# Pool queue in runs of sixteen gathers and sixteen scatters, first edge of equal nodes found by the merging matmul

## The chip, the cores and the metric

One NeuronCore of one Trainium2 chip, float32 throughout. The metric is the device time of one execution in microseconds; the median of three runs is given, and one further execution was profiled.

## The reference

A graph layer over N = 3125 nodes with 160 features and E = 53125 edges (random, sorted by `dst`; every edge has a `src` and a `dst` node). In short:

```
h   = relu(layernorm(x))                      # [N, 64 scalars + 32 vectors of 3]
s,v = h_s @ W_nl0,  einsum(h_v, W_nl1)
w   = relu(edge_attr_64 @ W_fc1) @ W_fc2      # per edge: w0..w4
xs, xv = s[dst], v[dst]                       # gather per edge
tp  = [w0*xs, w3*dot(xv,sh1), w1*xs*sh1, w2*xv, w4*cross(xv,sh1)]
agg = segment_sum(tp, src) / 32               # scatter-add per edge
out = x + gated( agg @ W_out_s + h_s @ W_skip0,  agg @ W_out_v + h_v @ W_skip1 )
```

The kernel applies `W_out_*` to each edge's products before the sum over `src`, so one edge adds a row of M = 192 floats.

## The kernel before

**Tiling.** Edges go in 416 tiles of 128; 4 tiles are a group (104 groups, index g, place j in a group), 2 groups a block (52 blocks, index b). All engines walk over the groups in software pipelines, each with its own written-out order of steps; DVE, PE and ACT have loops, the queues of POOL and SP are fully unrolled.

**POOL** (lines 376 to 417) only issues indirect DMAs in the main part: `gathers(b)` reads for every tile of a block 128 rows of 160 floats from `node_table` into one of 16 group slots `rows`; `scatters(b)` adds for every tile 128 rows of 192 floats into one of three DRAM tables `sums[t]` (three, so that a scatter waits only for the third one before it: one table has one scatter in flight). The order is 7 blocks of gathers first, then for each b: gathers of block b + 7 (8 of them), scatters of block b (8). After block 44 no gathers are left and the last 64 scatters follow one another. In every fourth block one of the eight gathers is left to SP, which reads its 128 rows by single-row DMAs.

**SP** (lines 280 to 340) loads, for each block, `from_col` and `from_row` (the `src` numbers of the block, the latter broadcast to all partitions, 512 KB), `ef` (edge features, 256 KB), and then issues 32 of those single-row reads (`gather_rows`, line 329) in blocks 0 to 47. `load_from(b)` waits for the indices of block b - 2 (`idx_ready`), because its buffers are double.

**DVE** (lines 794 to 930) makes the edge products from the gathered rows, adds the radial parts, and prepares the scatter. In a scatter, no row may occur twice: `same_nodes` builds per tile the 128x128 matrix `same` (line 872: equal `src` or not) and, by a second instruction (line 873, `before`), counts how many equal nodes stand before each edge. `repeats` and `rows_to_add` turn that into `add_idx`: the node for the first edge of equal nodes, a dump row for the others. `rows_to_add` (line 897) waits until the scatters that last used the index slot have landed (`added`), 8 groups earlier.

**PE** computes the hidden layers and the outputs, and `merge` (line 538) multiplies `same` with the messages, so that the first edge of equal nodes holds their sum. **ACT** copies PSUM results; `collect` (line 652) copies the merged sums into `to_add`, a ring of 8 groups, after the scatters that last used the slot have landed.

**At the end** SP reads the three tables back, and they are added, gated and stored.

Of the kernel before, what the change touches and what calls it, by code (L numbers as in the profile page):

```python
# [15 lines left out]
ALU = mybir.AluOpType  # L16
# [5 lines left out]
P = 128  # L22
N = 3125
E = 53125
S, V = 64, 32
# [37 lines left out]
W_LT = W_MC + 3 * V  # L63
W_DUMP = W_LT + P
W_END = W_DUMP + 1
# [19 lines left out]
EARLY_GROUPS = 2  # L85
AHEAD = 7
# [8 lines left out]
PER_BLOCK = [len(range(t, 2 * J, TABLES)) for t in range(TABLES)]  # L95
# [3 lines left out]
def table_of(b, p):  # L99

    turn = 2 * (b - DRAIN) if isinstance(b, int) and b > DRAIN else 0
    return (p + turn) % TABLES


def scattered(t, b, p):

    if isinstance(b, int) and b > DRAIN:
        return PER_BLOCK[t] * DRAIN + sum(table_of(k, q) == t for k in range(DRAIN, b + 1)
                                          for q in range(2 * J if k < b else p))
    return PER_BLOCK[t] * b + sum(q % TABLES == t for q in range(p))  # L110

# [35 lines left out]
def build_program(nc, x, wpack, edge_t, nodes_to, nodes_from, nodes_row, nodes_by_row, edge_vec, out):  # L147
# [3 lines left out]
    with ExitStack() as ctx:  # L151
# [11 lines left out]
        lower = w[:, W_LT:W_LT + P]  # L163
# [4 lines left out]
        spare = sb("spare", [P, max(NT * (S + M + 3 * V), UNROLL * J * (G_END + M))])  # L168
# [25 lines left out]
        msg = sb("msg", [P, 2, J, OUTS])  # L194
        radial = sb("radial", [P, 2, 2, 3 * V])
        same = sb("same", [P, 2, J, P])
        before = sb("before", [P, J, P])
        key = sb("key", [P, 3, 2, J])
        to_add_0 = sb("to_add_0", [P, UNROLL, J, M])
        to_add_1 = spare[:, UNROLL * J * G_END:UNROLL * J * (G_END + M)].rearrange(  # L200
# [5 lines left out]
        vec = msg[:, :, :, :].rearrange("p k j f -> p (k j f)")[:, 0:3 * TILES].rearrange("p (t i) -> p t i", i=3)  # L206
# [49 lines left out]
        def landed(b, u, j):  # L256

            p = u % 2 * J + j
            t = table_of(b, p)
            return t, 16 * scattered(t, b, p + 1)  # L260
# [6 lines left out]
        def _(sp):  # L267
# [95 lines left out]
        def _(pool):  # L363
# [29 lines left out]
            def scatters(b, v):  # L393

                for h in range(2):
                    pool.wait_ge(idx_ready, 2 * b + h + 1)
                    for j in range(J):
                        p = h * J + j
                        t = table_of(b, p)
                        if j % 2 == 0:  # L400
                            pool.wait_ge(sums_ready, 4 * b + 2 * h + 1 + j // 2)
                        if scattered(t, b, p) == 0:
                            pool.wait_ge(zeroed, 16 * (2 * len(ZERO_RUNS) + 1))
                        else:
                            pool.wait_ge(added[t], 16 * scattered(t, b, p))
                        pool.indirect_dma_start(  # L406
                            sums[t], bass.IndirectOffsetOnAxis(ap=add_idx[:, 2 * v + h, j:j + 1], axis=0),
                            to_add[2 * v + h][:, j, :], None, compute_op=ALU.add,
                        ).then_inc(added[t], 16)
# [4 lines left out]
            for b in range(BLOCKS):  # L414
                if b + AHEAD < BLOCKS:
                    gathers(b + AHEAD, (b + AHEAD) % ROWS_LOOP)
                scatters(b, b % LOOP)

        @block.tensor
        def _(pe):  # L420
# [107 lines left out]
            def merge(g, u, m):  # L528

                if not valid(g, GROUPS):  # L530
                    return
                pe.wait_ge(msg_ready, 2 * g + m + 1)
                if m == 0:
                    pe.wait_ge(same_ready, g + 1)
                if valid(g - 1, GROUPS) or m == 1:
                    pe.wait_ge(sums_ready, 2 * g + m)
                for q in range(2):
                    ins = nc.tensor.matmul(d_ps[:, q * M:(q + 1) * M], same[:, u % 2, 2 * m + q, :],  # L538
                                           msg[:, u % 2, 2 * m + q, 0:M], start=(q == 0), stop=(q == 1),
                                           skip_group_check=True)  # L540
                ins.then_inc(summed, 1)
# [35 lines left out]
        def _(act):  # L577
# [66 lines left out]
            def collect(g, u, m, b):  # L644
# [7 lines left out]
                nc.scalar.activation(to_add[u][:, 2 * m:2 * m + 2, :],  # L652
                                     d_ps[:, 0:2 * M].rearrange("p (q o) -> p q o", q=2),
                                     ACT.Copy).then_inc(sums_ready, 1)

            def step(i, u):
                g = RING * i + u
                u1, u2, u3 = (u - 1) % RING, (u - 2) % RING, (u - 3) % RING
                b3 = LOOP * i + (u - 3) // 2
# [3 lines left out]
                collect(g - 3, u3, 0, b3)  # L663
# [4 lines left out]
                collect(g - 3, u3, 1, b3)  # L668
# [28 lines left out]
        def _(dve):  # L697
# [78 lines left out]
            def vector_lengths():  # L776
# [8 lines left out]
                dve.wait_ge(rhat_ready, 1)  # L785

# [73 lines left out]
            def same_nodes(g, u, i):  # L860
# [5 lines left out]
                if valid(g - 2, GROUPS):  # L866
                    dve.wait_ge(summed, 2 * g - 2)
                    dve.wait_ge(idx_ready, g - 1)
                for j in range(J):
                    row = from_row[:, par, (h * J + j) * P:(h * J + j + 1) * P]  # L870
                    col = from_col[:, par, h * J + j:h * J + j + 1]
                    nc.vector.tensor_scalar(same[:, k, j, :], row, col, None, ALU.is_equal)  # L872
# [3 lines left out]
                nc.vector.tensor_scalar(key[:, 1, k, :], from_col[:, par, h * J:(h + 1) * J], -1.0,  # L876
                                        w[:, W_DUMP:W_DUMP + 1], ALU.mult, ALU.add).then_inc(same_ready, 1)

            def repeats(g, u):
                if not valid(g, GROUPS):  # L880
                    return
                k = u % 2
                dve.wait_ge(same_ready, g + 1)
                nc.vector.scalar_tensor_tensor(key[:, 2, k, :], key[:, 0, k, :], 0.5, key[:, 1, k, :],
                                               ALU.is_gt, ALU.mult).then_inc(repeats_ready, 1)

            def rows_to_add(g, u, b):

                if not valid(g, GROUPS):
                    return  # L890
                par, h, k = u // 2 % 2, u % 2, u % 2
                dve.wait_ge(repeats_ready, g + 1)
                if valid(g - RING, GROUPS):
                    for j in range(J - TABLES, J):
                        t, n = landed(b - LOOP, u, j)
                        dve.wait_ge(added[t], n)
                nc.vector.tensor_tensor(add_idx[:, u, :], key[:, 2, k, :], from_col[:, par, h * J:(h + 1) * J],  # L897
                                        ALU.add).then_inc(idx_ready, 1)

            def step(i, u):  # L900
                g = ROWS_RING * i + u
                u2 = (u - 2) % RING
# [7 lines left out]
                early = isinstance(g, int) and g - 2 < EARLY_GROUPS  # L910
                if not early:
                    same_nodes(g - 2, u2, 2 * i + (u - 2) // RING)
                radial_part(g - 2, u2, 1)
                if not early:
                    repeats(g - 2, u2)
                vectors(g - 2, u2, 1)
                if not early:
                    rows_to_add(g - 2, u2, 2 * LOOP * i + (u - 2) // 2)

            def early_group(g):  # L920
                same_nodes(g, g, 0)
                repeats(g, g)
                rows_to_add(g, g, g // 2)

            early_group(0)
# [3 lines left out]
            early_group(1)  # L929
# [5 lines left out]
            for u in range(SKEW, GROUPS % ROWS_RING + TAIL - 2):  # L935
                step(GROUPS // ROWS_RING, u)
# [41 lines left out]
def pack_weights(skip0, skip1, nl0, nl1, fc1, fc2, out_s, out_v):  # L978
# [34 lines left out]
    put(0, W_LT, np.tril(np.ones((P, P), np.float32), -1))  # L1013
    w[:, W_DUMP] = NPAD + np.arange(P)
    return w
# [40 lines left out]
```

## Time and profile before

| | us |
|---|---|
| median of 3 runs (1382.02 to 1385.59) | 1385.2 |
| profiled execution | 1387.66 |
| its span | 1385.8 |
| POOL busy | 1066.5 |
| PE busy / DVE busy / ACT busy | 919.5 / 880.1 / 428.5 |

The span is the time from the first to the last recorded instruction. Busy time of POOL is the time inside its DMA instructions; each is preceded by about 0.3 us that count as idle, so start-to-start distances say more than busy times. "idle before <-X" names what the engine had waited for last; "issue" means nothing that the profile shows.

### The profile page before, as it was taken

The numbers are of one execution on the slowest core, as the hardware profiler recorded it, in microseconds if no ns is written. First come the engines' busy times: TensorE is split into PE (matmuls) and PEld (weight loads), VectorE is DVE, ScalarE is ACT, GpSimd is POOL, SyncE is SP. The second block draws the span as 40 slices with busy tenths as digits, with TensorE's granted clock in tenths as the row PEclk, the third lists the DMA queues.
The fourth block names the chain that finished last, engine by engine and source line by source line (L and its number), as shares of the span: only waits on it lengthen the run. The fifth ranks groups of instructions, "written<-read, shape, count | busy, mean of one in ns | idle before, by whom it ended". The sixth has DMA issues, their size and how long they took to land.

```text
span 1385.8 us, 26047 instructions
## 1 busy us (share of the span) xinstructions
PE 919.5 (66%) x5648; PEld 780.3 (56%) x5648; DVE 880.1 (64%) x3693; ACT 428.5 (31%) x839; POOL 1066.5 (77%) x830
## 2 busy tenths in 40 slices
PE   7498766757757768577677675776766757769103
PEld 5387655646646657466566574665655646658102
DVE  7899747657566576575675766656647667579105
ACT  5154332322323323223233232232332323325101
POOL 1777788888888888888878888788788887887880
PEclk9699877786877877778778787787787877779556
DMA  9635555555454555554555555545554555456557
GB/s 351 165 92 102 105 80 86 99 80 105 81 80 105 78 84 101 80 105 80 80 105 80 88 97 81 104 79 82 105 78 88 97 80 106 79 78 90 52 55 274
DMA packets 124075, 139.89 MB, mean 101 GB/s; under 512 B 34241, under 2 KB 99585, under 8 KB 123970
## 3 DMA queue, kind: packets, MB, share of 16 engines
q0 software_dynamic: 79296, 74.04, 38.2%
q1 hardware_dynamic: 44674, 64.92, 15.1%
q14 instruction: 97, 0.79, 0.2%
q8 instruction: 8, 0.13, 0.0%
HBM read 86.24 MB, written 52.66 MB: 100 GB/s over the span
## 4 chain that ended last, share of the span: by engine, by line
DMA 31%; POOL 26%; DVE 23%; issue 14%; PE 3%; DVEq 2%; ACT 0%; POOLq 0%; SPq 0%; ACTq 0%
DMA sums<-to_add,add_idx 15%; DMA sums<-spare,add_idx 15%; POOL turn_space L388 9%; POOL sums L406 8%; DVE products_space L805 6%; POOL rows L388 5%; POOL spare L388 5%; DVE products_space L834 4%; DVE before L873 2%; DVE same L872 2%; DVE products_space L832 2%; DVE products_space L831 2%; DVE radial L847 1%; DVE msg L858 1%; DVE turn_space L816 1%
## 5 line engine op out<-in xcount | busy, mean ns | idle before, releaser
L507 PE MATMUL t_ps<-w,products_space 128*128 128x128 f32 (+1 forms) x1248 | 225.2, 312 | 350.6 <-DVE products_space L834 350.6
L523 PEld LDWEIGHTS o_ps<-w,pT 128*128 128x128 f32 (+1 forms) x2496 | 360.5, 223 | 40.7 <-issue 37.9
L406 POOL DMA_INDIRECT sums<-to_add,add_idx x208 | 326.6, 1570 | 67.9 <-issue 47.3
L507 PEld LDWEIGHTS t_ps<-w,products_space 128*128 128x128 f32 (+1 forms) x1248 | 166.3, 160 | 373.7 <-issue 335.8
L523 PE MATMUL o_ps<-w,pT 128*128 128x96 f32 (+1 forms) x2496 | 376.6, 309 | 0.0
L406 POOL DMA_INDIRECT sums<-spare,add_idx x208 | 326.6, 1570 | 64.4 <-issue 46.0
L631 ACT ACTIVATE pT<-t_ps 128x512 f32<-128x512 f32 (+1 forms) x312 | 185.4, 594 | 320.2 <-PE t_ps L507 319.7
L897 DVE TENSOR_TENSOR add_idx<-key,from_col 128x4 int32<-128x4 f32 x104 | 16.9, 163 | 371.0 <-DMA sums<-spare,add_idx 206.7
L388 POOL DMA_INDIRECT turn_space<-node_table,to_idx x186 | 187.1, 1006 | 56.7 <-issue 46.7
L640 ACT ACTIVATE msg<-o_ps 128x448 f32<-128x448 f32 x208 | 113.0, 543 | 335.8 <-PE o_ps L523 327.4
L538 PE MATMUL d_ps<-msg,same 128*128 128x192 f32 x832 | 197.0, 365 | 28.4 <-ACT spare L652 20.6
L538 PEld LDWEIGHTS d_ps<-msg,same 128*128 128x128 f32 x832 | 153.2, 217 | 60.9 <-issue 60.9
L388 POOL DMA_INDIRECT rows<-node_table,to_idx x112 | 114.2, 1020 | 41.3 <-issue 27.4
L491 PE MATMUL w_ps<-w,hid 64*128 64x224 f32 x832 | 145.4, 482 | 0.7 <-ACT hid L623 0.7
L873 DVE SCALAR_TENSOR_TENSOR before<-from_row,from_col,w 128x128 f32<-128x128 int32 x416 | 142.9, 343 | 0.0
L388 POOL DMA_INDIRECT spare<-node_table,to_idx x106 | 105.7, 997 | 32.4 <-issue 25.7
L872 DVE TENSOR_SCALAR same<-from_row,from_col 128x128 f32<-128x128 int32 x416 | 126.3, 305 | 0.0
L491 PEld LDWEIGHTS w_ps<-w,hid 64*128 64x128 f32 x832 | 93.9, 245 | 31.4 <-issue 26.6
L652 ACT ACTIVATE spare<-d_ps 128x384 f32<-128x384 f32 x104 | 51.1, 491 | 128.3 <-DMA sums<-spare,add_idx 105.3
L847 DVE TENSOR_TENSOR radial<-msg,rhat 128x192 f32<-128x192 f32 x208 | 72.5, 349 | 26.5 <-ACT msg L640 26.5
L805 DVE TENSOR_TENSOR products_space<-turn_space,rhat 128x256 f32<-128x256 f32 (+2 forms) x240 | 78.4, 392 | 3.5 <-issue 1.3
L652 ACT ACTIVATE to_add<-d_ps 128x384 f32<-128x384 f32 x104 | 51.1, 491 | 72.3 <-DMA sums<-to_add,add_idx 57.1
(96 smaller groups left out, 865.6 us busy)
## 6 DMA issues: line engine op xcount, KB each, us to landing
from_row<-nodes_row SPq DMA_DIRECT2D x52, 512.0 KB
ef<-edge_t SPq DMA_DIRECT2D x52, 256.0 KB
turn_space<-node_table SPq DMA_DIRECT2D x768, 0.6 KB
spare<-node_table SPq DMA_DIRECT2D x768, 0.6 KB
turn_space<-sums SPq DMA_DIRECT2D x9, 480.0 KB, 7.0
sums<-zeros SPq DMA_DIRECT2D x6, 672.0 KB, 9.2
sums<-to_add,add_idx POOLq DMA_INDIRECT x208, 3.6
sums<-spare,add_idx POOLq DMA_INDIRECT x208, 3.6
```

The costliest lines, as they stand in the source:

```text
L388: pool.indirect_dma_start(rows[2 * v + h][:, j, SC:CR], None, table, bass.IndirectOffsetOnAxis(ap=to_idx[:, (2 * b + h) * J + j:(2 * b + h ...
L406: pool.indirect_dma_start(sums[t], bass.IndirectOffsetOnAxis(ap=add_idx[:, 2 * v + h, j:j + 1], axis=0), to_add[2 * v + h][:, j, :], None, ...
L491: ins = nc.tensor.matmul(w_ps[m][:, q * NFC2:(q + 1) * NFC2], hid[half, par, cols], w[half, W_FC2:W_FC2 + NFC2], start=(q == 0), stop=(q = ...
L507: ins = nc.tensor.transpose(t_ps[(3 * u + c) % 2][0:ROWS[c], j * P:(j + 1) * P], prod[:, u % 2, j, a:e], ident)
L523: ins = nc.tensor.matmul(o_ps[m][:, base + oc:base + oc + n], pT[c][u % 2][:, cols], w[0:ROWS[c], wc:wc + n], start=(q == 0 and c == 0), s ...
L538: ins = nc.tensor.matmul(d_ps[:, q * M:(q + 1) * M], same[:, u % 2, 2 * m + q, :], msg[:, u % 2, 2 * m + q, 0:M], start=(q == 0), stop=(q ...
L631: nc.scalar.activation(pT[c][u % 2][:], t_ps[(3 * u + c) % 2][0:ROWS[c], :], ACT.Copy).then_inc(pT_ready, 1)
L640: nc.scalar.activation(msg[:, u % 2, 2 * m:2 * m + 2, :], o_ps[m][:, 0:2 * OUTS].rearrange("p (q o) -> p q o", q=2), ACT.Copy).then_inc(ou ...
L652: nc.scalar.activation(to_add[u][:, 2 * m:2 * m + 2, :], d_ps[:, 0:2 * M].rearrange("p (q o) -> p q o", q=2), ACT.Copy).then_inc(sums_read ...
L805: ins = nc.vector.tensor_tensor(vecs(crs[:, dst, :, i0 * V:(i0 + n) * V], n), vecs(rows[u][:, :, VE + v0 * V:VE + (v0 + n) * V], n), unit( ...
L872: nc.vector.tensor_scalar(same[:, k, j, :], row, col, None, ALU.is_equal)
L873: nc.vector.scalar_tensor_tensor(before[:, j, :], row, col, lower, ALU.is_equal, ALU.mult, accum_out=key[:, 0, k, j:j + 1])
```

## The change

1. **POOL order.** Blocks are taken in runs of two: gathers of blocks run + 7 and run + 8 (sixteen, or fifteen where SP takes one), then the scatters of blocks run and run + 1 (sixteen). The rotation over the three tables continues inside a run and restarts at each run.
2. **SP.** Before the loads of block b + 1, from b = 5 on, SP waits until all scatters of a whole run have landed: `scatters_landed((b - 5) // 2 * 2 + 1)`. `load_from(b)` itself waits for `same_ready` in place of `idx_ready`.
3. **First edge.** The `before` instructions are gone. A column of ranks, 3^(63-p) for edge p, stands ahead of each message; `merge` multiplies 193 columns in place of 192, `collect` copies the summed rank along, and `repeats` compares it with twice the edge's own rank. `repeats` and `rows_to_add` move from g - 2 to g - 4 in the step of DVE, and `rows_to_add` no longer waits for `added`.
4. `to_add` has 16 + 192 floats for each row; scatters read its last 192.

```diff
-            for b in range(BLOCKS):
-                if b + AHEAD < BLOCKS:
-                    gathers(b + AHEAD, (b + AHEAD) % ROWS_LOOP)
-                scatters(b, b % LOOP)
+            for run in range(0, BLOCKS, RUN):
+                for b in range(run + AHEAD, min(run + AHEAD + RUN, BLOCKS)):
+                    gathers(b, b % ROWS_LOOP)
+                for b in range(run, run + RUN):
+                    scatters(b, b % LOOP)
...
+            def scatters_landed(b):
+
+                for t in range(TABLES):
+                    sp.wait_ge(added[t], 16 * scattered(t, b, 2 * J))
+
             for b in range(BLOCKS):
+                if b + 1 < BLOCKS and b > LOOP:
+                    scatters_landed((b - LOOP - 1) // RUN * RUN + RUN - 1)
                 if b + 1 < BLOCKS:
                     load_from(b + 1, (b + 1) % 2)
...
                 if valid(b - 2, BLOCKS):
-                    sp.wait_ge(idx_ready, 2 * b - 2)
+                    sp.wait_ge(same_ready, 2 * b - 2)
...
-                    nc.vector.scalar_tensor_tensor(before[:, j, :], row, col, lower, ALU.is_equal, ALU.mult,
-                                                   accum_out=key[:, 0, k, j:j + 1])
...
             def repeats(g, u):
...
+                dve.wait_ge(sums_ready, 2 * g + 2)
+                nc.vector.scalar_tensor_tensor(key[:, 1, u % UNROLL, :], to_add[u][:, :, SUM_AT - 1],
+                                               w[:, W_FIRST:W_FIRST + 1], key[:, 0, u % UNROLL, :],
+                                               ALU.is_le, ALU.mult).then_inc(repeats_ready, 1)
...
-                if valid(g - RING, GROUPS):
-                    for j in range(J - TABLES, J):
-                        t, n = landed(b - LOOP, u, j)
-                        dve.wait_ge(added[t], n)
-                nc.vector.tensor_tensor(add_idx[:, u, :], key[:, 2, k, :], from_col[:, par, h * J:(h + 1) * J],
-                                        ALU.add).then_inc(idx_ready, 1)
+                nc.vector.tensor_scalar(add_idx[:, u, :], key[:, 1, u % UNROLL, :], -1.0, w[:, W_DUMP:W_DUMP + 1],
+                                        ALU.mult, ALU.add).then_inc(idx_ready, 1)
```

## Rows read from the trace of the kernel before

**Rows 1.** The page's first lines: span, and busy time of each engine (share, instructions).
```profile
span 1385.8 us, 26047 instructions
PE 919.5 (66%) x5648; PEld 780.3 (56%) x5648; DVE 880.1 (64%) x3693; ACT 428.5 (31%) x839; POOL 1066.5 (77%) x830
```

**Rows 2.** Part 5, POOL's DMA instructions: count, busy us, mean ns, idle before, releaser.
```profile
L406 POOL DMA_INDIRECT sums<-to_add,add_idx x208 | 326.6, 1570 | 67.9 <-issue 47.3
L406 POOL DMA_INDIRECT sums<-spare,add_idx x208 | 326.6, 1570 | 64.4 <-issue 46.0
...
L388 POOL DMA_INDIRECT turn_space<-node_table,to_idx x186 | 187.1, 1006 | 56.7 <-issue 46.7
...
L388 POOL DMA_INDIRECT rows<-node_table,to_idx x112 | 114.2, 1020 | 41.3 <-issue 27.4
```

**Rows 3.** The view of waits: us in total, times, longest.
```profile
DVE add_idx L897 <- DMA sums<-spare,add_idx: 206.7, 25, 9.7
```

**Rows 4.** Timeline of POOL: start, us, line, tile, idle before; first, turnarounds, last.
```profile
36.07 1.15 POOL L388 DMA_INDIRECT rows<-node_table,to_idx  x1 [7.48 <-DMA node_table<-spare]
...
614.10 1.56 POOL L406 DMA_INDIRECT sums<-spare,add_idx  x1 [0.30 <-issue]
615.97 1.02 POOL L388 DMA_INDIRECT spare<-node_table,to_idx  x1 [0.30 <-DMA sums<-spare,add_idx]
...
625.08 1.61 POOL L406 DMA_INDIRECT sums<-to_add,add_idx  x1 [0.30 <-issue]
...
640.15 1.02 POOL L388 DMA_INDIRECT turn_space<-node_table,to_idx  x1 [0.30 <-DMA sums<-to_add,add_idx]
...
650.63 1.62 POOL L406 DMA_INDIRECT sums<-to_add,add_idx  x1 [0.30 <-issue]
...
1350.01 1.55 POOL L406 DMA_INDIRECT sums<-spare,add_idx  x1 [0.30 <-issue]
```

**Rows 5.** The view of line 406: from a scatter's issue to its landing.
```profile
DMA to landing us min/median/max: 3.5/3.6/7.8
```

**Rows 6.** Timeline of SP's queue: the loads of two following blocks, and a late one.
```profile
108.71 0.42 SPq L289 DMA_DIRECT2D from_row<-nodes_row  x1
...
110.99 14.37 SPq L329 DMA_DIRECT2D turn_space<-node_table  x32
...
125.83 0.45 SPq L289 DMA_DIRECT2D from_row<-nodes_row  x1
...
646.47 0.43 SPq L289 DMA_DIRECT2D from_row<-nodes_row  x1
```

**Rows 7.** Windows of 1 us after the load at 618.82: engines' busy, PEclk, DMA share, GB/s.
```profile
622.00:623.00 1.00, 1.00 (x6) 1.00 (x5) 1.00 (x3) 0.58 (x1) 0.69 (x2) 0.63 0.95 344
...
626.00:627.00 1.00, 1.00 (x10) 0.72 (x11) 1.00 (x7) 0.71 (x2) 0.69 (x1) 1.00 0.02 4
```

**Rows 8.** Timeline of POOL around the load at 125.83.
```profile
125.68 1.56 POOL L406 DMA_INDIRECT sums<-to_add,add_idx  x1 [0.30 <-DMA sums<-to_add,add_idx]
...
129.41 1.56 POOL L406 DMA_INDIRECT sums<-to_add,add_idx  x1 [0.30 <-issue]
133.52 1.56 POOL L406 DMA_INDIRECT sums<-to_add,add_idx  x1 [2.55 <-DMA sums<-to_add,add_idx]
```

**Rows 9.** Timeline in the last 64 scatters: two loads and the stalls behind them.
```profile
1247.18 0.43 SPq L289 DMA_DIRECT2D from_row<-nodes_row  x1
...
1252.98 1.69 POOL L406 DMA_INDIRECT sums<-to_add,add_idx  x1 [1.22 <-ACT to_add L652]
...
1263.04 0.43 SPq L289 DMA_DIRECT2D from_row<-nodes_row  x1
...
1269.16 1.55 POOL L406 DMA_INDIRECT sums<-spare,add_idx  x1 [1.29 <-DMA sums<-spare,add_idx]
```

**Rows 10.** The removed instruction on the page, and once beside a gather.
```profile
L873 DVE SCALAR_TENSOR_TENSOR before<-from_row,from_col,w 128x128 f32<-128x128 int32 x416 | 142.9, 343 | 0.0
...
644.16 0.40 DVE L873 SCALAR_TENSOR_TENSOR before<-from_row,from_col,w 128x128 f32<-128x128 int32 x1
644.24 0.95 POOL L388 DMA_INDIRECT turn_space<-node_table,to_idx  x1 [0.30 <-issue]
```

More of the change, by code:

```diff
@@ L62 @@
 W_MC = W_MB + 3 * V
-W_LT = W_MC + 3 * V
-W_DUMP = W_LT + P
-W_END = W_DUMP + 1
+W_DUMP = W_MC + 3 * V
+W_RANK = W_DUMP + 1
+W_FIRST = W_RANK + 1
+W_END = W_FIRST + 1
 NA = W_NC - W_NA
@@ L85 @@
 EARLY_GROUPS = 2
+SUM_AT = 16
+SUM_ROW = SUM_AT + M
 AHEAD = 7
@@ L92, with scattered_in_runs @@
 TAIL = 4
-PER_BLOCK = [len(range(t, 2 * J, TABLES)) for t in range(TABLES)]
+RUN = 2
+PER_RUN = [len(range(t, RUN * 2 * J, TABLES)) for t in range(TABLES)]
 DRAIN = BLOCKS - AHEAD
 def table_of(b, p):
-    turn = 2 * (b - DRAIN) if isinstance(b, int) and b > DRAIN else 0
+    turn = 2 * (b % RUN) if b <= DRAIN else 2 * (DRAIN % RUN + b - DRAIN)
     return (p + turn) % TABLES
 def scattered(t, b, p):
[L107 to L110, printed above, removed]
+    return sum(table_of(k, q) == t for k in range(b + 1) for q in range(2 * J if k < b else p))
+def scattered_in_runs(t, run, place):
+    return PER_RUN[t] * run + sum(q % TABLES == t for q in range(place))
 def last_place(t):
@@ L193, in build_program @@
         pT = [[sb(f"pT{c}{k}", [ROWS[c], GE]) for k in range(2)] for c in range(3)]
-        msg = sb("msg", [P, 2, J, OUTS])
+        ranked = sb("ranked", [P, 2, J, 1 + OUTS])
+        msg = ranked[:, :, :, 1:1 + OUTS]
         radial = sb("radial", [P, 2, 2, 3 * V])
         same = sb("same", [P, 2, J, P])
[L197 to L200, printed above, removed]
+        key = sb("key", [P, 2, UNROLL, J])
+        to_add_0 = sb("to_add_0", [P, UNROLL, J, SUM_ROW])
+        to_add_1 = spare[:, UNROLL * J * G_END:UNROLL * J * (G_END + SUM_ROW)].rearrange(
             "p (u j m) -> p u j m", u=UNROLL, j=J)
@@ L254, in build_program, with landed @@
         gates = to_add_0[:, :, :, :].rearrange("p u j m -> p (u j m)")[:, 0:NT * SO].rearrange("p (t s) -> p t s", s=SO)
[L256 to L260, printed above, removed]
+        def landed(run, u, j):
+            place = u % (2 * RUN) * J + j
+            if isinstance(run, int) and run > DRAIN // RUN:
+                b, p = divmod(run * RUN * 2 * J + place, 2 * J)
+                t = table_of(b, p)
+                return t, 16 * scattered(t, b, p + 1)
+            t = place % TABLES
+            return t, 16 * scattered_in_runs(t, run, place + 1)
         out_sb = rows_0[:, :, :, :].rearrange("p u j f -> p (u j f)")[:, 0:NT * F].rearrange("p (t f) -> p t f", t=NT)
@@ L537, in merge @@
                 for q in range(2):
-                    ins = nc.tensor.matmul(d_ps[:, q * M:(q + 1) * M], same[:, u % 2, 2 * m + q, :],
-                                           msg[:, u % 2, 2 * m + q, 0:M], start=(q == 0), stop=(q == 1),
+                    ins = nc.tensor.matmul(d_ps[:, q * (1 + M):(q + 1) * (1 + M)], same[:, u % 2, 2 * m + q, :],
+                                           ranked[:, u % 2, 2 * m + q, 0:1 + M], start=(q == 0), stop=(q == 1),
                                            skip_group_check=True)
@@ L642, in copy_outputs, with collect @@
                                      ACT.Copy).then_inc(out_copied, 1)
-            def collect(g, u, m, b):
+            def collect(g, u, m, run):
                 if not valid(g, GROUPS):
@@ L649, in collect @@
                     for j in (2 * m, 2 * m + 1):
[L650 removed]
+                        t, n = landed(run - LOOP // RUN, u, j)
                         act.wait_ge(added[t], n)
[L652 to L653 removed]
+                nc.scalar.activation(to_add[u][:, 2 * m:2 * m + 2, SUM_AT - 1:SUM_ROW],
+                                     d_ps[:, 0:2 * (1 + M)].rearrange("p (q o) -> p q o", q=2),
                                      ACT.Copy).then_inc(sums_ready, 1)
@@ L658, in step @@
                 u1, u2, u3 = (u - 1) % RING, (u - 2) % RING, (u - 3) % RING
-                b3 = LOOP * i + (u - 3) // 2
+                run = LOOP // RUN * i + (u - 3) // (2 * RUN)
                 copy_turned(g - 1, u1, 0)
@@ L662, in step @@
                 copy_turned(g - 1, u1, 1)
-                collect(g - 3, u3, 0, b3)
+                collect(g - 3, u3, 0, run)
                 copy_outputs(g - 2, u2, 1)
@@ L667, in step @@
                     hidden(LOOP * i + u // 2 + 1, (u // 2 + 1) % 2)
-                collect(g - 3, u3, 1, b3)
+                collect(g - 3, u3, 1, run)
             hidden(0, 0)
@@ L867, in same_nodes @@
                     dve.wait_ge(summed, 2 * g - 2)
-                    dve.wait_ge(idx_ready, g - 1)
+                if valid(g - UNROLL, GROUPS):
+                    dve.wait_ge(repeats_ready, g - UNROLL + 1)
                 for j in range(J):
-                    row = from_row[:, par, (h * J + j) * P:(h * J + j + 1) * P]
-                    col = from_col[:, par, h * J + j:h * J + j + 1]
-                    nc.vector.tensor_scalar(same[:, k, j, :], row, col, None, ALU.is_equal)
-                    nc.vector.scalar_tensor_tensor(before[:, j, :], row, col, lower, ALU.is_equal, ALU.mult,
-                                                   accum_out=key[:, 0, k, j:j + 1])
-                nc.vector.tensor_scalar(key[:, 1, k, :], from_col[:, par, h * J:(h + 1) * J], -1.0,
+                    nc.vector.tensor_scalar(same[:, k, j, :], from_row[:, par, (h * J + j) * P:(h * J + j + 1) * P],
+                                            from_col[:, par, h * J + j:h * J + j + 1], None, ALU.is_equal)
+                nc.vector.tensor_scalar(key[:, 0, u % UNROLL, :], from_col[:, par, h * J:(h + 1) * J], -1.0,
                                         w[:, W_DUMP:W_DUMP + 1], ALU.mult, ALU.add).then_inc(same_ready, 1)
@@ L934, in _ @@
                     step(i, u)
-            for u in range(SKEW, GROUPS % ROWS_RING + TAIL - 2):
+            for u in range(SKEW, GROUPS % ROWS_RING + TAIL):
                 step(GROUPS // ROWS_RING, u)
```

39 lines of the change are left out of this document (14 added, 25 removed).

## The prediction

> **What bounds the kernel now.** I read the busy times first [rows 1]: POOL leads with 1066.5 us, but 77% of a span bounds nothing by itself. The reader is to see why it does here in POOL's timeline [rows 4]: from the gather at 36.07 to the end of the scatter at 1350.01 + 1.55 = 1351.6, POOL issues one indirect DMA after another, each 0.30 us behind the one before. The 254 us that count as idle in these 1315.5 us are almost all that fixed 0.30. The page's groups [rows 2] give the pieces: 416 scatters of 1570 ns, 404 gathers of about 1008 ns (the third group, into the tile spare, is like the two shown). With the gap, an undisturbed scatter takes 1.55 + 0.30 = 1.86 us from start to start (the last scatter's duration in [rows 4]) and an undisturbed gather 0.95 + 0.30 = 1.25 [rows 10]. 416 x 1.86 + 404 x 1.25 = 1279; POOL's stretch is 1315.5, so all disturbances together are worth 36 us. That is the most that a new order of the same DMAs could win, and it is the account on which the change books.
>
> The waits agree: DVE stands 206.7 us at the index instruction for the landing of scatters out of the tile spare alone, half of the ring [rows 3], so compute runs ahead until the ring of eight groups is full and is then released by POOL. Ahead of 36 and after 1351.6 (34 us of reading back and finishing) nothing of the change matters: its additions there are one column instruction.
>
> **The change part by part.** Sums are against the profiled 1387.66 us (span 1385.8); the median of the runs is 2.5 lower, and I apply the difference to the median.
>
> *DVE without `before`, indices two groups later, one column more in merge and collect.* 416 x 343 ns = 143 us leave DVE [rows 10]. DVE waits for POOL, so the wait grows by as much: 0. The cover is POOL's pace of about 51 us for two blocks (625.08 to 650.63 is one [rows 4]). Do the later indices come in time? The indices of a run need DVE two groups beyond it, and those need the slots that the scatters two runs earlier give back. From that landing POOL has a run of gathers, a run of scatters and a second run of gathers before it asks for them, 20 + 30 + 20 = 70 us, for some four group steps on DVE; DVE's busy time is at most 880.1 / 104 = 8.5 us a group with `before` [rows 1], so 34 us. Cost 0; if the cover failed, each run would wait for the rest of a step. The ring still holds two runs, so the double buffer stays whole. Gathers of block run + 8 now wait for the products of block run, made before the previous run was collected: 0.
>
> *POOL, turnarounds removed.* Gather runs and scatter runs alternate 45 times before, 23 times after: 22 pairs fewer. The first gather after scatters takes 1.02 (615.97, 640.15), against 0.95; the first scatter after gathers 1.61 and 1.62, against 1.55 [rows 4]. The second of each run is still about 0.03 long. Per pair 0.07 + 0.07 + 0.03 + 0.03 and some hundredths of gaps: 0.23, so 22 x 0.23 = -5.1 us. Bounds 0 (the excess belongs to other traffic and stays) and -6.
>
> *The held loads, first of a pair.* I count from the start L of the last scatter of a run. It lands at L + 3.6 [rows 5]; SP then issues `from_col` and, 0.4 us later, `from_row`: L + 4.15. The first gather starts at L + 1.87 (614.10 to 615.97), so this load meets the third gather, as loads do now. 0.
>
> *The second of the pair.* Both loads of a pair wait for the same run, so the second goes when SP is through with the first block: its 32 single-row reads hold SP (14.37 us), and from load to load it needs 125.83 - 108.71 = 17.1 us where nothing delays it [rows 6]; I allow up to 0.5 more, since the reads wait for their register loads. That is L + 21.3 to 21.7. The first scatter of the next run comes after sixteen gathers: the eight from 640.15 to 650.63 took 10.48 [rows 4], twice that less a turnaround is 20.8, so L + 22.7; after fifteen, 1.3 earlier: L + 21.4. **So the second load is issued exactly at the turn to scatters**, 1.2 us ahead of the first scatter or level with it. Before, the latest one came 650.63 - 646.47 = 4.2 us ahead [rows 4, 6], and left no mark. A load's traffic fills the queues from about 1 to 5 us behind its issue: 0.95 of the DMA engines and 344 GB/s at 622 to 623, for the load of 618.82, and 4 GB/s at 626 to 627 [rows 7].
>
> What does a scatter pay beside such traffic? The trace has three cases. Issued at 125.68, with a load at 125.83, it let the third after it start at 133.52 instead of 131.27: 2.25 us late [rows 8]. The loads at 1247.18 and 1263.04 have stalls of 1.22 and 1.29 behind them, 0.92 and 0.99 beyond the usual 0.30 [rows 9]. A scatter has three starts, 5.6 us, to land in and needs 3.6 of them, so 2 us of delay are free.
> - Fifteen gathers, level with the load: 10 pairs. The three cases say 0.9 to 2.25; only light gathers stand ahead of this scatter where scatters stood there, which speaks for the lower end. I take 1.1: +11. Bounds 0 and 22.5.
> - Sixteen gathers, 1.2 us behind the load: 11 pairs. By then part of the load is through; the nearest rows are 0 (4.2 us) and 2.25 (level). I take 0.1, since the free 2 us should cover most: +1.1. Bounds 0 and 25.
>
> *Opening.* Load 5 at 125.83 falls into scatters now. After, the first scatter stands behind 71 gathers rather than 63, at about 130, and DVE, freed of 1.7 us a group, asks for the load no later: it falls among gathers. The stall of 2.25 goes: -2.2 (bounds 0, -2.3).
>
> *Last 64 scatters.* No gathers are left to hide loads in. Before, two loads met scatters; after, three do (49 by SP's pace, 50 and 51 together once block 45 has landed): one more of the same price, +1.2 (bounds 0 and +4, as two loads close together may cost more).
>
> *Sum:* -5.1 - 2.2 + 11 + 1.1 + 1.2 = +6.0. From 1385.2: **1391 us**.
>
> Two rules of the Trainium skill bear on this. "DMA: Bandwidth & Descriptors" (Queues, rings and completion order) says that each DMA engine takes packets in turn from the queues that have work; by it a scatter is delayed by no more than the load itself has to move, so the price per pair is bounded and cannot grow into a long stall, which the three cases bear out. "SBUF — State Buffer" says that a DVE instruction with two SBUF inputs contends with a GpSimd instruction that reads SBUF; by it the removed `before`, which reads `from_row` and the mask, would have been lengthening POOL's DMAs.
>
> **The rivals.**
>
> *A, the second load costs nothing* (faster). Place: the turn to scatters. If the load's issue slips by a microsecond or its traffic is mostly through when the first scatter's rows move, every delay stays under the free 2 us. For it: loads 4.2 us ahead leave no mark, and the pair with sixteen gathers is on its way there. Against: three of three loads issued among scatters cost something. Then -5.1 - 2.2 and about +1 at the end: 1379. It decides where a scatter lands within 5.6 us.
>
> *B, every pair pays the full price.* 21 x 2.25 = 47, less 7.3, plus 2: 1427. For it: the case at 125.68 has just this phase with `ef` behind it. Against: the two smaller cases, and the sixteen's lead.
>
> *C, the removed `before` had slowed POOL.* POOL's busy time is above its undisturbed one by 416 x 0.02 + 404 x 0.06 = 32 us [rows 2, 10], some of it the turnarounds. Of DVE's time with two inputs from SBUF, `before` is about a quarter, so up to 8 us: 1383, and 1371 together with A. Against: the gather at 644.24 takes 0.95 with a `before` at 644.16 beside it [rows 10]. The rule of the Trainium skill on two SBUF inputs, above, stands behind this rival.
>
> *D, the indices or loads come late,* and POOL waits within a period: some us a run, 1400 or more. Against: 70 us for 34.
>
> *E, long runs turn no cheaper*, with the collisions as small as in A: 1384, no change.
>
> **How the numbers follow.** Forecast 0.45 (1386 to 1403 by its own bounds of 0.5 to 2.25 for the fifteens), A 0.30, B 0.04, C 0.07, D 0.04, E 0.10. A measurement here tells 0.3% (4.2 us) from no change, so faster means below 1381, slower above 1389.4. Faster: A and most of C, 0.34. Same: E, the rest of C, and the lower edge of the forecast (0.07): 0.20. Slower: the other 0.38 of the forecast, B and D: 0.46. The range takes in A and the forecast's bound: 1374 to 1403.
>
> **What would show it.** In the timeline of POOL: runs of 16 scatters, `from_row` loads in pairs 17 to 18 us apart, the second within 1.5 us of a run's first scatter; idle before the fourth scatter of a run above 0.30, mostly after fifteen gathers. Landing times of up to 7 us for first scatters. First gathers of 1.02 and first scatters of 1.61 half as often. DVE busy about 175 us less (143 and the reads of its accumulator), its wait moved from the index instruction to one for ACT. Wrong would be: no stall beyond 0.30 from 160 to 1230 us (then A), POOL durations shorter inside runs (C), or waits of POOL for DVE's indices (D).

## The result and the profile after

The changed kernel takes 1390.9 us (median of 6 runs, 1389.7 to 1394.0), the kernel before 1384.8 beside it (6 runs): ratio 1.0046, 95% interval 1.0031 to 1.0061. The forecast was 1391. The profiled execution took 1390.5 with a span of 1388.7, which is 2.8 us above the profiled one of before (the spans are 2.9 apart); the rest of the 6.1 us between the medians lies within the spread of single executions.

The page's first lines and POOL's groups of the changed kernel (columns as in [rows 1, 2]):

```profile
span 1388.7 us, 25040 instructions
PE 859.2 (62%) x5648; PEld 718.0 (52%) x5648; DVE 770.2 (55%) x2862; ACT 423.1 (30%) x839; POOL 1067.2 (77%) x830
...
L422 POOL DMA_INDIRECT sums<-to_add,add_idx x208 | 332.2, 1597 | 71.1 <-issue 39.2
L422 POOL DMA_INDIRECT sums<-spare,add_idx x208 | 333.7, 1604 | 65.5 <-issue 37.5
L404 POOL DMA_INDIRECT turn_space<-node_table,to_idx x186 | 182.1, 979 | 56.7 <-issue 56.1
L404 POOL DMA_INDIRECT rows<-node_table,to_idx x112 | 109.9, 981 | 41.3 <-issue 33.5
```

DVE has lost 110 us and PE 60, and nothing came of it. POOL's busy time is the same, 1067.2 against 1066.5, but not its parts: a gather is 29 ns shorter on the mean, a scatter 30 ns longer. (Each busy time here is that of one execution; the same kernel had 1068.0 in another, and such pairs differ by about 1 us.) Both engines that lost work only stand longer; DVE's wait is no longer that of [rows 3] but for PE, and PE's for the held loads (the view of waits; us, times, longest):

```profile
PE hid_ps L489 <- DMA ef<-edge_t: 392.1, 46, 17.2
```

The turn from gathers to scatters in the timeline, first SP's queue and then POOL, for a run with fifteen gathers ahead:

```profile
620.72 0.43 SPq L298 DMA_DIRECT2D from_row<-nodes_row  x1
...
623.01 14.38 SPq L338 DMA_DIRECT2D spare<-node_table  x32
637.59 0.37 SPq L297 DMA_DIRECT2D from_col<-nodes_from  x1
638.00 0.48 SPq L298 DMA_DIRECT2D from_row<-nodes_row  x1
```

```profile
637.44 1.62 POOL L422 DMA_INDIRECT sums<-to_add,add_idx  x1 [0.31 <-issue]
639.36 1.58 POOL L422 DMA_INDIRECT sums<-to_add,add_idx  x1 [0.30 <-issue]
641.24 1.76 POOL L422 DMA_INDIRECT sums<-to_add,add_idx  x1 [0.30 <-issue]
644.08 1.55 POOL L422 DMA_INDIRECT sums<-to_add,add_idx  x1 [1.07 <-DMA sums<-to_add,add_idx]
```

The pair of loads is 17.3 us apart (620.72, 638.00), and the second goes 0.6 us behind the first scatter. The chain of waits gives that scatter's landing (start, us from issue):

```profile
637.44 6.37 DMA sums<-to_add,add_idx
```

6.4 us instead of 3.6, more than the three starts it has, and the fourth scatter begins 0.77 late. This repeats every 101 us, once in two runs: ten such stalls between 200 and 1230 us, at 238.74, 339.88 and so on to 1150.73, 0.3 to 1.0 us each beyond the usual 0.30, 7.6 us together. All ten follow fifteen gathers; none of the eleven runs after sixteen has one. After sixteen, the second load is 0.9 us ahead of the first scatter (688.02 and 688.93). It is felt there too, but not paid for: from 200 to 1230 us the first scatter of a run lands 5.8 to 6.5 us behind its start after fifteen gathers and 4.6 to 5.4 after sixteen, and a scatter has 5.6 before POOL needs it.

### The profile page after: what moved, and what is told of

Same layout as the page of the kernel before. It is cut to its first block, busy times and chain, and to the rows that moved or that the text cites. A ratio compares the mean times of both kernels' runs of the same rounds, so it can differ in the third digit from the quotient of the medians.

```text
span 1388.7 us, 25040 instructions
## 1 busy us (share of the span) xinstructions
PE 859.2 (62%) x5648; PEld 718.0 (52%) x5648; DVE 770.2 (55%) x2862; ACT 423.1 (30%) x839; POOL 1067.2 (77%) x830
## 4 chain that ended last, share of the span: by engine, by line
DMA 41%; POOL 37%; issue 13%; PE 5%; DVE 2%; ACT 1%; SPq 1%; POOLq 0%; DVEq 0%; ACTq 0%
DMA sums<-to_add,add_idx 20%; DMA sums<-spare,add_idx 18%; POOL sums L422 15%; POOL turn_space L404 11%; POOL spare L404 6%; POOL rows L404 6%; DMA ef<-edge_t 2%; PE hid_ps L489 1%; PE w_ps L508 1%; PE d_ps L555 1%; PE o_ps L540 1%; DMA spare<-sums 1%; PE w_ps L588 0%; ACT ranked L657 0%; PE t_ps L524 0%
## 5 line engine op out<-in xcount | busy, mean ns | idle before, releaser
L489 PE MATMUL hid_ps<-ef,w 128*128 128x512 f32 x104 | 86.5, 926 | 392.1 <-DMA ef<-edge_t 392.1
L540 PE MATMUL o_ps<-w,pT 128*128 128x96 f32 (+1 forms) x2496 | 325.2, 281 | 0.0
L540 PEld LDWEIGHTS o_ps<-w,pT 128*128 128x128 f32 (+1 forms) x2496 | 308.0, 195 | 31.8 <-issue 29.0
L489 PEld LDWEIGHTS hid_ps<-ef,w 128*128 128x128 f32 x104 | 21.1, 253 | 403.1 <-DMA ef<-edge_t 403.0
L555 PE MATMUL d_ps<-ranked,same 128*128 128x193 f32 x832 | 199.1, 368 | 27.1 <-ACT spare L669 13.0
L555 PEld LDWEIGHTS d_ps<-ranked,same 128*128 128x128 f32 x832 | 156.4, 217 | 75.5 <-issue 70.5
L657 ACT ACTIVATE ranked<-o_ps 128x448 f32<-128x448 f32 x208 | 112.9, 543 | 215.7 <-PE o_ps L540 215.6
L640 ACT ACTIVATE hid<-hid_ps 128x512 f32<-128x512 f32 x52 | 31.4, 604 | 382.9 <-PE hid_ps L489 382.9
L850 DVE TENSOR_TENSOR products_space<-w_ps,turn_space 128x192 f32<-128x192 f32 x96 | 33.3, 347 | 200.0 <-PE w_ps L508 200.0
L866 DVE TENSOR_TENSOR radial<-ranked,rhat 128x192 f32<-128x192 f32 x208 | 72.9, 351 | 111.2 <-ACT ranked L657 110.9
L669 ACT ACTIVATE spare<-d_ps 128x386 f32<-128x386 f32 x104 | 51.2, 493 | 137.1 <-DMA sums<-spare,add_idx 120.7
```

The source lines that it names most:

```text
L489: nc.tensor.matmul(hid_ps[:], w[:, W_FC1:W_FC1 + P], ef[:, par, :], start=True, stop=True).then_inc(fc1_done, 1)
L540: ins = nc.tensor.matmul(o_ps[m][:, base + oc:base + oc + n], pT[c][u % 2][:, cols], w[0:ROWS[c], wc:wc + n], start=(q == 0 and c == 0), s ...
L555: ins = nc.tensor.matmul(d_ps[:, q * (1 + M):(q + 1) * (1 + M)], same[:, u % 2, 2 * m + q, :], ranked[:, u % 2, 2 * m + q, 0:1 + M], start ...
L657: nc.scalar.activation(msg[:, u % 2, 2 * m:2 * m + 2, :], o_ps[m][:, 0:2 * OUTS].rearrange("p (q o) -> p q o", q=2), ACT.Copy).then_inc(ou ...
L669: nc.scalar.activation(to_add[u][:, 2 * m:2 * m + 2, SUM_AT - 1:SUM_ROW], d_ps[:, 0:2 * (1 + M)].rearrange("p (q o) -> p q o", q=2), ACT.C ...
L866: nc.vector.tensor_tensor(radial[:, m].rearrange("p q (i k) -> p q i k", i=3), msg[:, u % 2, 2 * m:2 * m + 2, Q:OUTS].unsqueeze(2).broadca ...
```

## The experiments

Each kernel is compared with the kernel before on its own chip. The first four ran on a chip on which every engine stood for tens of microseconds without a recorded reason, above all in the opening; the view of waits of e1_pair_first from 30 to 200 us begins

```profile
PEld t_ps L533 <- issue: 75.8, 8, 40.5
ACT ranked L666 <- remote: 54.0, 1, 54.0
DVE radial L875 <- issue: 41.9, 2, 38.7
```

waits that the profile puts down to no work of the kernel (remote: what ended it is not told). The kernel before took 1413.9 there. I draw nothing from these four, and repeated three of them beside the changed kernel on another chip.

**e1 and e1b, both loads of a pair first.** The edit in SP's loop:

```diff
+            for b in range(LOOP + 1, BLOCKS, RUN):
+                for k in range(b, min(b + RUN, BLOCKS)):
+                    loads(k)          # the wait, load_from(k + 1), load_features(k + 2)
+                for k in range(b, min(b + RUN, BLOCKS)):
+                    gather_rows(k)
```

> The changed kernel, with SP issuing the loads of both blocks of a pair first and the single-row reads of both after them, so that the second load follows the first by about 3 us and falls among gathers. Theory (the second load collides with the first scatters of a run): the ten stalls of 0.6 to 1.3 us before the fourth scatter go (7.6 us beyond the usual 0.30), and the first scatter of a run is back from 1.72 to 1.62 (2 us more): 1391 becomes 1380 to 1384, below the kernel before. Rival (the stalls come from the longer runs themselves): they stay, 1389 to 1392.

On the disturbed chip 1469.0 (ratio 1.039). Again, beside the changed kernel itself:

> The changed kernel itself, unaltered, beside the others on one chip, since on the chip of the first four runs every engine showed waits of tens of us for its own instructions. If this chip is as the first one was: ratio 1.003 to 1.006 to the kernel before, POOL busy 1067, ten stalls of 0.6 to 1.3 us.

> Both loads of a pair first, as in e1. Theory (the second load collides with the first scatters): 7 to 10 us below the changed kernel on this chip, no stall over 0.2 us beyond the usual gap in the steady part. Rival (stalls belong to long runs): the same as the changed kernel. Second rival: without the first of the two loads held apart, PE gets its features earlier and works beside the gathers instead of the scatters, and POOL's instructions stretch there instead: the sum of POOL's busy time stays at 1067.

Measured: the changed kernel 1394.3 (ratio 1.0058, 1.0035 to 1.0081), e1b 1383.6 (0.9989, 0.9978 to 1.0000): 10.7 us less. POOL's waits for landings from 200 to 1230 us (the view of waits; us, times, longest), in the changed kernel

```profile
POOL sums L422 <- DMA sums<-to_add,add_idx: 22.1, 51, 1.4
POOL sums L422 <- DMA sums<-spare,add_idx: 16.2, 53, 0.3
```

and in e1b:

```profile
POOL sums L431 <- DMA sums<-spare,add_idx: 16.5, 54, 0.3
POOL sums L431 <- DMA sums<-to_add,add_idx: 14.0, 46, 0.3
```

38.3 us in 104 waits is 7.1 beyond 0.30 each (38.9 in 103 and 8.0 in the first trace of the changed kernel; there are ten stalls in both, all after fifteen gathers); 30.5 in 100 is 0.5. The stalls are gone, by the order of the loads alone, with runs of sixteen as they were. The rival (stalls belong to long runs) falls. POOL busy fell too, by 2.5 us (1068.0 to 1065.5), little more than two executions of one kernel differ by (1066.6 in e1c), so the second rival's steady busy time is not excluded. The shorter first scatters expected of e1 did not come: 1.67 us on the mean in the changed kernel beside it, 1.71 in e1b.

**e2 and e2b, runs of eight** (`RUN = 1`; the merging code stays):

> The changed kernel with RUN = 1: the merging matmul finds the first edge as in the change, but POOL alternates eight gathers and eight scatters as before the change, and a load waits for the scatters of one block. Theory (the loss is all in the order of loads against runs of sixteen; the new first-edge code is free): no stalls in the steady part, 22 turnarounds back at 0.2 us each: 1384 to 1388, as the kernel before. Rival (the removed DVE instructions had slowed POOL): POOL busy falls by 5 to 8 us and the time to 1376 to 1380. Other rival (the later indices or the wider copy cost time): 1390 or more.

On the disturbed chip 1429.2 (ratio 1.0072).

> RUN = 1, as in e2. Theory: no stalls in the steady part, turnarounds back: 3 to 6 us below the changed kernel and level with the kernel before. Rival (the removed DVE instructions had slowed POOL): 10 us or more below the changed kernel, POOL busy under 1062.

Measured: 1394.4 (ratio 1.0074, 1.0047 to 1.0102), no faster than the changed kernel. Neither outcome named for e2b came; the time is that of the last rival of e2 (1390 or more), but not its cause, since POOL waits for no indices beyond 0.30 in the steady part. There are no stalls in the steady part, as expected, but POOL's instructions are longer:

```profile
PE 902.0 (65%) x5648; PEld 762.2 (55%) x5648; DVE 774.8 (56%) x2862; ACT 417.2 (30%) x839; POOL 1075.4 (77%) x830
```

1075.4 against 1066.5 before: 8.9 us. The two profiled executions are 4.8 us apart in span (POOL waits 2.6 less in e2b and the tail is 1.4 shorter), the medians 9.6. e2b has all of the change but POOL's order: the first-edge code with its later indices, the wider rows of `to_add` and SP's new waits. Together these, which I had booked at 0 for POOL, cost about 9 us by the medians when POOL's order is as before, although they take 105 us of work from DVE; which of them does it is not shown. The runs of sixteen give 7 to 8 us of busy time back (1075.4 to 1068.0 beside it, 1067.2 first), more than the 5.1 forecast for the turnarounds.

**e3, no hold** (the wait for a landed run removed):

> The changed kernel without the wait for a landed run ahead of SP's loads; the buffers' own waits stay. Theory (a load among scatters costs POOL 0.6 to 2.2 us): the loads then follow DVE, which works while scatters free the ring, so most of 44 loads fall into scatter runs: 1.0 to 1.5 us each in place of 0.8 for ten, 1420 to 1450. Rival (the hold itself is what costs, since PE stands 392 us waiting for features): 1380 to 1386.

Measured on the disturbed chip only: 1472.8 (ratio 1.040), beside 1469.0 of e1. It settles nothing, and what the hold itself is worth stays open.

**e4 and e4b, an instruction like `before` added back:**

```diff
                     nc.vector.tensor_scalar(same[:, k, j, :], ..., ALU.is_equal)
+                    nc.vector.scalar_tensor_tensor(unused[:, j, :], from_row[...], from_col[...], ident,
+                                                   ALU.is_equal, ALU.mult, accum_out=unused_key[:, k, j:j + 1])
```

> The changed kernel with an instruction like the removed one added back on DVE (two inputs from SBUF, 416 of 343 ns with the accumulator read, its result unused). Theory (DVE has slack and POOL does not notice it): 1390 to 1393, POOL busy within 1.5 us of 1067. Rival (DVE instructions with two SBUF inputs stretch POOL's DMA instructions): POOL busy 1071 to 1075, the time 1395 to 1400.

On the disturbed chip 1492.0 (ratio 1.052).

> The DVE instruction added back beside the merging matmul, as in e4. Theory (covered by DVE's slack): within 2 us of the changed kernel, POOL busy 1067 to 1069. Rival (two inputs from SBUF on DVE stretch POOL's DMA instructions): POOL busy 1071 to 1075 and the time 4 to 8 us above the changed kernel.

Measured: 1399.1 (ratio 1.0090, 1.0060 to 1.0120), 4.8 above the changed kernel by the medians (the profiled executions are 8.8 apart):

```profile
PE 854.0 (61%) x5648; PEld 712.3 (51%) x5648; DVE 879.2 (63%) x3694; ACT 421.7 (30%) x839; POOL 1076.9 (77%) x830
```

POOL busy 1076.9 against 1068.0: the rival's effect is there, even above its range. DVE had slack for this work and its wait absorbed it, and yet POOL's own instructions grew by 8.9 us. The next two ask which DVE work does it.

**e7, one input instead of two.** `same`'s comparison a second time into an unused tile, in place of the instruction of e4:

> The changed kernel with 416 DVE instructions added that have one tensor input from SBUF (a second copy of the comparison that builds same, result unused), where e4b added 416 with two, which raised POOL busy from 1068.0 to 1076.9. Theory (only instructions with two inputs from SBUF stretch POOL's DMA instructions): POOL busy 1065 to 1070, time within 3 us of the changed kernel (ratio 1.003 to 1.008). Rival (any added DVE work does, by lengthening and shifting its bursts): POOL busy 1073 to 1080, ratio 1.008 to 1.012.

Measured: 1398.3 (ratio 1.0091, 1.0070 to 1.0111):

```profile
PE 849.5 (61%) x5648; PEld 707.8 (51%) x5648; DVE 851.3 (61%) x3278; ACT 420.5 (30%) x839; POOL 1073.4 (77%) x830
```

81 us of one-input work go with 5.4 more on POOL (1068.0 to 1073.4, though the two profiles are of different chips), 109 us of two-input work went with 8.9: 0.07 and 0.08 us for each us of DVE work, the rival's figures. The timelines do not bear the rival out. Of e7's 5.4 us, 4.7 lie in the 71 gathers ahead of the first scatter, and 0.3 between there and the last 64 scatters; of e4b's 8.9, 8.7 lie in that middle part. What lies beside a POOL instruction tells them apart (two cases of the changed kernel):

```profile
581.89 0.61 DVE L853 TENSOR_TENSOR products_space<-w_ps,turn_space 128x192 f32<-128x192 f32 x2
581.92 0.94 POOL L404 DMA_INDIRECT spare<-node_table,to_idx  x1 [0.30 <-issue]
...
610.85 1.62 DVE L824 TENSOR_TENSOR products_space<-rows,rhat 128x256 f32<-128x256 f32 x5
611.01 1.68 POOL L422 DMA_INDIRECT sums<-spare,add_idx  x1 [0.30 <-DVE add_idx L910]
```

L853 reads `w_ps` from PSUM, so one of its inputs is in SBUF; both of L824's are. From 200 to 1220 us of the changed kernel, the first two instructions of each run set aside, 63 POOL instructions lie beside DVE instructions with at most one SBUF input alone: none is more than 0.02 us beyond 0.95 or 1.55 (the most is 0.011). Of 293 beside at least one with two, 113 are, and the mean excess of the 293 is 0.06. In e7 only 4 of 84 of the first kind are long, by 0.07. So in the steady part, as far as one trace of each tells, the theory holds and not the rival; e7's 5.4 us belong to the opening, and what does it there is not shown.

**e6, the kernel of e1 without the cross products** (five instructions of each group left out; the cross and dot products are zero), and **e1c**, its control:

> The kernel of e1 (both loads first) with the five cross-product instructions of each group left out on DVE, about 200 us of work with two inputs from SBUF; the cross products are then zero. Theory (POOL's DMA instructions are stretched beside such instructions): POOL busy falls from 1065.5 by 5 to 10 us, to 1056 to 1060, and the time by as much or more against e1 (1370 to 1378). Rival (the stretch comes with DMA traffic and loads): POOL busy 1064 to 1066, the time as e1.

> The kernel of e1 again, as the control for e6 and to narrow its interval against the kernel before. By e1b: ratio 0.998 to 1.000. The theory's sum (turnarounds saved, no stall in the steady part, POOL's stretches unchanged in sum) gives 4 to 5 us less than before at best, 0.9965; the rival (the merging code puts back what the turnarounds save) 0.999 to 1.001.

Measured: e6 1371.5 (ratio 0.9903, 0.9882 to 0.9924), e1c 1382.0 (0.9980, 0.9966 to 0.9994). First e6, then e1c:

```profile
PE 834.8 (61%) x5648; PEld 701.8 (51%) x5648; DVE 625.0 (46%) x2447; ACT 419.7 (31%) x839; POOL 1053.2 (77%) x830
```

```profile
PE 847.8 (61%) x5648; PEld 716.2 (52%) x5648; DVE 770.8 (56%) x2862; ACT 421.2 (30%) x839; POOL 1066.6 (77%) x830
```

146 us less on DVE (I had expected 200), 13.4 less on POOL (0.09 for 1; I had expected 5 to 10), and 10.6 us less time by the medians. The five left out are the two-input instructions of L824. An engine that is idle for half the span, and that POOL never waits for in the steady part, shortens the kernel when it works less. The profiled executions exaggerate this: by the medians, e4b, e7 (by the ratios) and e6 moved by 4.8, 4.6 and 10.6 us, 0.04 to 0.07 for each us of DVE work.

**e5, the second load later still.** The held loads of the second block of each pair are issued after 16 of its single-row reads:

```diff
                for n16, r in enumerate(range(r0, r0 + ROWS_PER_BLOCK, ROWS_PER_LOAD)):
+                    if n16 == 1:
+                        between()     # loads(b), for the second block of a held pair
```

> The changed kernel, with the second load of each held pair issued 16 single-row reads later (about 25 us behind the landing in place of 17.5), so that it falls among the third to fifth scatter of every run, after fifteen and after sixteen gathers alike. Theory (a load among scatters costs POOL 0.6 to 2.2 us, and sixteen gathers were spared because their second load came 1 us ahead of the first scatter): about 21 stalls instead of ten, 1 to 2 us each, 15 to 30 us above the changed kernel: ratio to the kernel before 1.016 to 1.028. Rival (the stall belongs to the turn from gathers to scatters, not to scatters in general): stalls vanish, ratio 0.998 to 1.001.

Measured: 1407.9 (ratio 1.0152, 1.0128 to 1.0176), 13 to 15 us above the changed kernel by the ratios. POOL's waits from 165 to 1230 us, and one of the stalls (the second row, 1.47 before it):

```profile
POOL sums L430 <- DMA sums<-to_add,add_idx: 28.7, 56, 1.8
...
POOL sums L430 <- DMA sums<-spare,add_idx: 23.6, 48, 2.0
```

```profile
554.86 1.56 POOL L430 DMA_INDIRECT sums<-to_add,add_idx  x1 [0.30 <-issue]
...
557.89 1.56 POOL L430 DMA_INDIRECT sums<-to_add,add_idx  x1 [1.47 <-DMA sums<-to_add,add_idx]
```

52.3 us in 104 waits, 21.1 beyond 0.30, in twenty stalls (four of them cost less than 0.4 us): now after sixteen gathers too. A load among scatters costs 1.04 us on the mean. The theory holds for the place and the number of the stalls; the time is just below the range I gave (1.016 to 1.028).

## Why the prediction was right, and where only its sum was

**The place of the loss** is as forecast: the second load of a pair is issued at the turn to scatters, 17.3 us behind the first, and the scatter level with it lands late. e1b takes the loss away; e5 doubles the number of stalls and nearly triples their sum (7.6 to 21.1). Rival A, no price, would have needed no stall; it had 0.30 from me and is refuted for the fifteens. For the sixteens its reason held: their landings stay under 5.6 us.

**Its size.** Fifteens: forecast 10 x 1.1 = 11, measured 7.6. Sixteens: forecast 1.1, measured 0. The price of 1.1 per collision was nearly that of e5 (1.04); at the turn itself it is 0.76; why it is lower there was not tried. Rival B, 2.25 for all, was out by a factor of six. The Trainium skill, "DMA: Bandwidth & Descriptors" (Queues, rings and completion order), has each DMA engine serve its queues in turn. The trace agrees roughly: the ten landings of 5.8 to 6.5 us are 2.2 to 2.9 more than usual, and the load's 768 KB at the 344 GB/s of [rows 7] would take 2.3 (an estimate); no long stall came.

**Turnarounds**, forecast -5.1: the effect exists. First and second instructions of a run are 1.02 and 0.97, and 1.62 and 1.58, in both kernels, with half as many runs; counted over 200 to 1220 us, the excess of these over 0.95 and 1.55 falls from 9.9 us for 80 turns to 6.2 for 40. That is -3.7, some -4.1 for all. But POOL's busy time did not fall by it, and this is the step that failed: I had put the removed DVE work and the shifted steps at exactly 0 for POOL. With the turns set aside, POOL's excess in the same window rose from 14.3 to 16.4 us, and in the gathers ahead of the first scatter from 4.9 (63) to 6.8 (71). Before, DVE was at work beside all 230 gathers of the window (mean excess 0.05) and beside 121 of 246 scatters (0.01); now it is beside 115 of 270 gathers (0.02) and 241 of 284 scatters (0.06). Beside DVE at rest it is 0.00 for gathers (there were none before) and 0.008 or less for scatters, in both kernels. DVE's work moved from the gathers to the scatters, and did not cost less there.

**Opening**, forecast -2.2: the stall of [rows 8] is gone, as stated. **Last 64 scatters**, forecast +1.2: one stall of 2.1 us at 1274.34, behind loads at 1266.44 and 1268.20, in place of four with 3.2 together ([rows 9] shows two of them, and I had booked only those): -1.0, so wrong in sign by a small amount. Loads 50 and 51 together cost what I feared for them, but load 49 cost nothing.

**The sum** of the profiled executions: stalls +7.6 - 2.2 - 1.0 = +4.4 and POOL busy +0.7 make +4.9 in POOL's stretch with rounding, of which a tail shorter by 1.6 and a start earlier by 0.4 leave the 2.9 by which the span grew. The forecast had +13.3 for stalls and -7.3 for gains, together +6.0. Two errors cancelled: the stalls were too dear by 6.7 us (13.3 against 7.6 - 1.0) and POOL's busy time too cheap by 5.8 (-5.1 against +0.7). The interval of the measured ratio (+4 to +8 us) holds +4.9 and +6.0. That the median came out at the very 1391 of the forecast is luck; the place of the loss and its sign are not.

**Two signs missed.** DVE's busy time was to fall by about 175 us and fell by 110: 143 and the 32 of the accumulator reads are sums over instructions that overlap, which the busy time counts once. And DVE's wait was to move to one for ACT; it moved to PE (401 us for `w_ps`, 111 for ACT), since PE stands for the held loads, a wait that the prediction did not have.

**Rival C** had 0.07 and deserved more, though not in its own form. Its mechanism is real: DVE work with two SBUF inputs stretches POOL's DMA instructions, 0.08 and 0.09 us per us in the profiles of e4b and e6. It did not pay here, because POOL's instructions in the old order are 8.9 us longer with the rest of the change (e2b), where 105 us less DVE work should have given 8 less. I took one gather of 0.95 beside one `before` [rows 10] for the rule. It was not far off for that instruction: in e4b's steady part (200 to 1220 us) POOL instructions beside the added work but not beside the products of the gathered rows with `rhat` (its L825, L824 in the changed kernel) have a mean excess of 0.04 us (103 of them), while those beside the products of `rhat` went from 0.09 in the changed kernel (100) to 0.13 (118). Most of e4b's rise came about by what the added work pushed together. The Trainium skill, "SBUF — State Buffer" (SBUF: two separate sides), names DVE instructions with two SBUF inputs, or in a mode that uses both ports, as those that can hold POOL up. In the steady part the traces agree: 63 POOL instructions beside one-input work without a stretch, and 113 stretched of 293 beside two-input work. Whether the comparison of e7 uses both ports no run here shows.

**What stays open:** why the rest of the change in runs of eight lengthens POOL's instructions by 9 us, of which 7.1 lie between the first scatter and the last 64. Its DVE instructions last as long as before. The bursts lie otherwise against POOL's instructions, and `same` is made by four comparisons in a row; neither was tried apart, nor were SP's waits. What the hold is worth is open too (e3), and so is e7's opening.

**D and E:** POOL did not wait for indices beyond 0.30 us in the steady part, so D fell; E is what the busy times say, though for another reason than I gave.

**A version ahead of both:** the kernel of e1, with both loads first: 0.9989 and 0.9980 of the kernel before on two chips, the first interval reaching 1 (0.9978 to 1.0000), the second below it (0.9966 to 0.9994), and 0.993 of the changed kernel. That is ahead by 0.1 to 0.2%, no more.

## What to carry to other kernels

When a queue is a chain of DMA instructions without gaps, list what each wait for a landing leaves free (here 2 us) and look where the big loads of the other queue fall once the order changes: a load held for an event is not enough if a second one follows it at the queue's own pace. And do not book work on an engine with slack at nothing before you have asked whether the bottleneck's own instructions are shorter when that engine rests: group their durations by what runs beside them, all of them, not one, and by where that work reads. Compare also where in the span a busy time grew: e4b and e7 look alike in their totals and not in their timelines.

## What the runs showed of the hardware

- A DMA instruction of POOL takes 0.95 us (gather of 128 rows) or 1.55 (adding scatter) when DVE rests, to 0.03 us; beside DVE work it is up to 0.8 us longer (e7). On the mean POOL's busy time moved by 0.07 to 0.09 us in the profiles, and the time by 0.04 to 0.07 in the medians, for each us of DVE work added or taken away (e4b, e6, e7).
- The stretch comes beside DVE instructions with two inputs in SBUF (113 of 293 by more than 0.02 us in the changed kernel's steady part), not beside those with one input there and the other in PSUM or absent (0 of 63; in e7 4 of 84, by 0.07).
- The first two of a run of gathers take 1.02 and 0.97, the first two of a run of scatters 1.62 and 1.58: 0.2 us for a change of kind.
- A load of 768 KB issued beside an adding scatter delays its landing from 3.6 us to between 5.8 and 6.5 (the ten turns after fifteen gathers); issued 0.4 to 1.2 us ahead of it, to between 4.6 and 5.4 (the ten after sixteen).
- One chip made the same programs 29 us (the kernel before) to 93 us (e4) slower, by waits without a recorded reason; there e1 was slower than e2 (1469.0 and 1429.2), elsewhere faster (1383.6 and 1394.4).
